# Channel attention with its weights turned and applied to v, and the output weights applied after

## What is computed

```
q = jnp.einsum('bse,ef->bsf', x, Wq)
k = jnp.einsum('bse,ef->bsf', x, Wk)
v = jnp.einsum('bse,ef->bsf', x, Wv)
qT = jnp.swapaxes(q, 1, 2)
kT = jnp.swapaxes(k, 1, 2)
vT = jnp.swapaxes(v, 1, 2)
attn_scores = jnp.einsum('bes,bfs->bef', qT, kT) / np.sqrt(HEAD_DIM)
attn_weights = jax.nn.softmax(attn_scores, axis=-1)
attn_output = jnp.einsum('bef,bfs->bes', attn_weights, vT)
attn_output = jnp.swapaxes(attn_output, 1, 2)
return jnp.einsum('bse,ef->bsf', attn_output, Wo)
```

## Time and profile before

| | us |
|---|---|
| median of 3 executions (lowest, highest) | 1319.75 (1319.05, 1320.85) |
| the profiled execution | 1320.28 |
| its span, first to last instruction | 1318.3 |
| TensorE busy in it | 1182.8 (90%) |
| VectorE, ScalarE, GpSimd busy | 774.4, 580.5, 603.9 |

### The profile page before, as it was taken

How to read it: one execution, slowest core, us unless ns; L and a number is a source line. 1 busy time by engine, 2 the same in 40 slices (tenths; PEclk the granted TensorE clock), 3 DMA queues, 4 the chain that set the end, 5 groups by cost and what they waited for, 6 DMA issues and landing times. The chain is left out here.

```text
span 1318.3 us, 24667 instructions
## 1 busy us (share of the span) xinstructions
PE 1182.8 (90%) x7421; PEld 831.5 (63%) x7422; DVE 774.4 (59%) x1930; ACT 580.5 (44%) x1504; POOL 603.9 (46%) x752
## 2 busy tenths in 40 slices
PE   7997889967989869978999999999999759999995
PEld 5774556544555534446888888888888536666663
DVE  4553688865887749955667767767666422222221
ACT  3432676643333300016656766666676323333331
POOL 2001465533655537636556666656665112232322
PEclk9998999988999979979999999999999869999998
DMA  7000000002998030041000000000002212222323
GB/s 259 0 0 12 14 18 12 13 1 81 187 206 170 1 154 12 0 188 72 5 13 13 13 15 15 20 12 12 12 17 77 85 43 42 47 44 44 47 41 88
DMA packets 46354, 69.41 MB, mean 53 GB/s; under 512 B 4736, under 2 KB 42672, under 8 KB 45232
## 3 DMA queue, kind: packets, MB, share of 16 engines
q1 hardware_dynamic: 37136, 52.95, 15.1%
q0 software_dynamic: 7152, 9.34, 4.4%
q10 hardware_dynamic: 2000, 6.29, 1.3%
HBM read 57.12 MB, written 32.58 MB: 68 GB/s over the span
## 5 line engine op out<-in xcount | busy, mean ns | idle before, releaser
L1742 PE MATMUL ga.pkq<-ga.xnT,g.early 128*128 128x128 f32 x1280 | 157.0, 276 | 1.0 <-ACT ga.halves L1660 1.0
L1742 PEld LDWEIGHTS ga.pkq<-ga.xnT,g.early 128*128 128x128 f32 x1280 | 151.6, 193 | 9.6 <-issue 8.2
L1522 POOL TENSOR_TENSOR ga.halves<-ga.halves,g.ga_sinT 128x512 f32<-128x512 f32 x80 | 103.3, 1291 | 51.6 <-ACT ga.halves L1660 51.6
L1786 PE MATMUL ga.turn_out<-g.early,ga.aT 128*128 128x256 f32 x512 | 118.3, 385 | 0.3 <-ACT ga.aT L1682 0.3
L1667 ACT ACTIVATE ga.e<-ga.psc,ga.negmax 128x128 f32<-128x128 f32 x256 | 90.6, 366 | 46.9 <-DVE ga.negmax L1588 45.9
L1530 POOL TENSOR_TENSOR ga.kqT<-ga.by_cos,ga.halves 128x512 f32<-128x512 f32 x80 | 102.6, 1283 | 16.5 <-issue 16.5
L1786 PEld LDWEIGHTS ga.turn_out<-g.early,ga.aT 128*128 128x128 f32 x512 | 95.9, 192 | 12.7 <-ACT ga.aT L1682 0.7
L1897 DVE TENSOR_TENSOR ex.hidden<-ex.silu,ex.p 128x512 f32<-128x512 f32 x39 | 26.8, 687 | 124.3 <-PE ex.p L1950 117.9
L1575 DVE TENSOR_TENSOR ga.by_cos<-ga.pkq,g.ga_cosT 128x512 f32<-128x512 f32 x80 | 55.3, 691 | 72.5 <-PE ga.pkq L1742 44.6
L1767 PE MATMUL ga.paT<-ga.pT,ga.v 128*128 128x512 f32 x128 | 68.4, 617 | 12.3 <-ACT ga.pT L1675 9.1
L1945 PE MATMUL ex.p<-g.spare,ex.xnT 128*128 x156 | 76.9, 616 | 1.1 <-ACT ex.xnT L1925 0.8
(11 more groups left out here) (290 smaller groups left out, 2630.2 us busy)
## 6 DMA issues: line engine op xcount, KB each, us to landing
mo_rows<-in_pad_rows SPq DMA_DIRECT2D x1, 18447.0 KB, 101.4
ex.row<-mo_rows SPq DMA_DIRECT2D x39, 129.0 KB, 2.1
g.spare<-in_mo_w SPq DMA_DIRECT2D x1, 4096.0 KB, 12.1
g.late<-in_mo_w SPq DMA_DIRECT2D x1, 4096.0 KB, 22.7
g.early<-in_mo_w SPq DMA_DIRECT2D x1, 4096.0 KB, 12.4
g.ctxT<-in_ctxR SPq DMA_DIRECT2D x1, 2048.0 KB, 11.9
xa.ctxT<-in_ctxT SPq DMA_DIRECT2D x16, 128.0 KB, 2.5
g.spare<-cv_rows SPq DMA_DIRECT2D x1, 2048.0 KB, 8.0
```

Source lines behind the costliest of these rows:

```text
L1522: nc.gpsimd.tensor_tensor(by_sin[:, par, :].rearrange("p (h t) -> p h t", h=REP), halves[:, par, :].rearrange("p (h t) -> p h t", h=REP), ...
L1742: last = nc.tensor.matmul(pkq[:, par, j * P:(j + 1) * P], w[:, q, at * P:(at + 1) * P], xnT[:, s.par, q, :], start=(q == 0), stop=(q == C ...
L1786: last = nc.tensor.matmul(pout, aT[:, h // REP, (h % REP) * P:(h % REP + 1) * P], g.ga_wo[:, h, :], start=(h == 0), stop=(h == H - 1))
```

## The change

The product over `f` is now taken with v first. After the exponentials of batch s-1, TensorE turns the 256x256 matrix `w` in four transposes into the new PSUM tile `pwT`, and VectorE copies it to `wT` (128x512, one instruction). One step later TensorE multiplies `wT` and `vT` into `pmix` (now attention output by channel, four matmuls of 128 columns); ScalarE scales its rows by the inverted sums into `mixed` (two instructions of 128x128); then TensorE multiplies `mixed` by the output weights into `pout`. Gone are the product `w` x `wo`, VectorE's scaling of the output weights and the 128x512 copy `mix`.

```diff
--- before.py
+++ after.py
@@ -264,21 +264,21 @@
         xnT = m.sb("xnT", [P, 2, C, P])
         qk = m.sb("qk", [P, 2, 2 * D])
         vT = m.sb("vT", [P, 2, C, P])
-        w = m.sb("w", [P, 2, C, D])
+        w, wT = m.sb("w", [P, 2, C, D]), m.sb("wT", [P, 2, C, D])
         negmax, rowsum = m.sb("negmax", [P, 2, C]), m.sb("rowsum", [P, 2, C])
-        wo = m.sb("wo", [P, 2, C, D])
-        mix = m.sb("mix", [P, 2, C, D])
+        mixed = m.sb("mixed", [P, 2, C, P])
         turn = m.ps("turn", [P, 512])
         pqk = m.ps("pqk", [P, 2 * D])
         pv = m.ps("pv", [P, 512])
         psc = m.ps("psc", [P, C, D])
-        pmix = m.ps("pmix", [P, C, D])
+        pwT = m.ps("pwT", [P, C, D])
+        pmix = m.ps("pmix", [P, 512])
         pout = m.ps("pout", [P, 512])
         (var_ready, rstd_ready, xn_ready, turned, xnT_ready, qk_done, qk_ready, vT_done, vT_ready, scores_done,
-         max_ready, w_ready, wo_ready, mix_done, mix_ready, out_done, x_added) = map(m.sem, (
+         max_ready, w_ready, sum_ready, w_turned, wT_ready, mix_done, mix_ready, out_done, x_added) = map(m.sem, (
             "var_ready", "rstd_ready", "xn_ready", "turned", "xnT_ready", "qk_done", "qk_ready", "vT_done",
-            "vT_ready", "scores_done", "max_ready", "w_ready", "wo_ready", "mix_done", "mix_ready", "out_done",
-            "x_added"))
+            "vT_ready", "scores_done", "max_ready", "w_ready", "sum_ready", "w_turned", "wT_ready", "mix_done",
+            "mix_ready", "out_done", "x_added"))
         g.finished = m.sems
         scale = 8 ** -0.5
         block = ctx.enter_context(nc.Block())
@@ -341,16 +341,18 @@
                 b = s.back(1)
                 if b.on:
                     dve.wait_ge(w_ready, upto(b))
-                    nc.vector.reciprocal(rowsum[:, b.par, :], rowsum[:, b.par, :])
-                    dve.drain()
-                    if b.base is None and b.n == 0:
-                        dve.wait_ge(g.ca_o_loaded, 16)
+                    nc.vector.reciprocal(rowsum[:, b.par, :], rowsum[:, b.par, :]).then_inc(sum_ready, 1)
+                if s.on:
+                    dve.wait_ge(vT_done, upto(s))
+                    if s.past(2):
+                        dve.wait_ge(mix_done, upto(s, back=2))
+                    nc.vector.tensor_copy(vT[:, s.par, :, :], pv[:, 0:D]).then_inc(vT_ready, 1)
+                b = s.back(1)
+                if b.on:
+                    dve.wait_ge(w_turned, upto(b))
                     if b.past(2):
                         dve.wait_ge(mix_done, upto(b, back=2))
-                    for c in range(C):
-                        last = nc.vector.tensor_scalar(wo[:, b.par, c, :], g.ca_wo[:, c, :], rowsum[:, b.par, c:c + 1],
-                                                       None, ALU.mult)
-                    last.then_inc(wo_ready, 1)
+                    nc.vector.tensor_copy(wT[:, b.par, :, :], pwT[:]).then_inc(wT_ready, 1)
                 b = s.back(-2)
                 if b.on and b.base is None and b.n in X_PARTS:
                     dve.wait_ge(g.x_loaded[X_PARTS.index(b.n)], 16)
@@ -359,11 +361,6 @@
                     if b.past(2):
                         dve.wait_ge(xn_ready, upto(b, back=2))
                     layer_norm_stats(nc, m, g.x[:, b.i, :], b.par, var_ready)
-                if s.on:
-                    dve.wait_ge(vT_done, upto(s))
-                    if s.past(2):
-                        dve.wait_ge(out_done, upto(s, back=2))
-                    nc.vector.tensor_copy(vT[:, s.par, :, :], pv[:, 0:D]).then_inc(vT_ready, 1)
             steps(dve, step, 2, 2)
 
         @block.scalar
@@ -374,11 +371,22 @@
                     if s.past(2):
                         act.wait_ge(vT_done, upto(s, back=2))
                     nc.scalar.activation(xnT[:, s.par, :, :], turn[:, 0:D], ACT.Copy).then_inc(xnT_ready, 1)
+                b = s.back(2)
+                if b.on:
+                    act.wait_ge(mix_done, upto(b))
+                    act.wait_ge(sum_ready, upto(b))
+                    if b.past(2):
+                        act.wait_ge(out_done, upto(b, back=2))
+                    for c in range(C):
+                        last = nc.scalar.activation(mixed[:, b.par, c, :], pmix[:, c * P:(c + 1) * P], ACT.Copy,
+                                                    scale=rowsum[:, b.par, c:c + 1])
+                    last.then_inc(mix_ready, 1)
                 b = s.back(1)
                 if b.on:
                     act.wait_ge(max_ready, upto(b))
                     if b.past(2):
-                        act.wait_ge(mix_done, upto(b, back=2))
+                        act.wait_ge(w_turned, upto(b, back=2))
+                        act.wait_ge(mix_ready, upto(b, back=2))
                     for c in range(C):
                         last = nc.scalar.activation(w[:, b.par, c, :], psc[:, c, :], ACT.Exp, bias=negmax[:, b.par, c:c + 1],
                                                     scale=scale, accum_out=rowsum[:, b.par, c:c + 1])
@@ -388,11 +396,6 @@
                     if s.past(2):
                         act.wait_ge(scores_done, upto(s, back=2))
                     nc.scalar.activation(qk[:, s.par, :], pqk[:], ACT.Copy).then_inc(qk_ready, 1)
-                if b.on:
-                    act.wait_ge(mix_done, upto(b))
-                    if b.past(2):
-                        act.wait_ge(out_done, upto(b, back=2))
-                    nc.scalar.activation(mix[:, b.par, :, :], pmix[:], ACT.Copy).then_inc(mix_ready, 1)
             steps(act, step, 0, 2)
 
         @block.tensor
@@ -418,14 +421,15 @@
                     last.then_inc(scores_done, 1)
                 b = s.back(2)
                 if b.on:
-                    pe.wait_ge(mix_ready, upto(b))
+                    pe.wait_ge(wT_ready, upto(b))
                     pe.wait_ge(vT_ready, upto(b))
                     if b.past(1):
-                        pe.wait_ge(x_added, upto(b, back=1))
+                        pe.wait_ge(mix_ready, upto(b, back=1))
                     for c in range(C):
-                        last = nc.tensor.matmul(pout[:, 0:D], vT[:, b.par, c, :], mix[:, b.par, c, :],
-                                                start=(c == 0), stop=(c == C - 1))
-                    last.then_inc(out_done, 1)
+                        for f in range(C):
+                            last = nc.tensor.matmul(pmix[:, c * P:(c + 1) * P], wT[:, b.par, f, c * P:(c + 1) * P],
+                                                    vT[:, b.par, f, :], start=(f == 0), stop=(f == C - 1))
+                    last.then_inc(mix_done, 1)
                 if s.on:
                     pe.wait_ge(xnT_ready, upto(s))
                     if s.base is None and s.n == 0:
@@ -435,6 +439,18 @@
                     for c in range(C):
                         last = nc.tensor.matmul(pqk[:], xnT[:, s.par, c, :], g.ca_wqk[:, c, :], start=(c == 0), stop=(c == C - 1))
                     last.then_inc(qk_done, 1)
+                b = s.back(2)
+                if b.on:
+                    pe.wait_ge(mix_ready, upto(b))
+                    if b.base is None and b.n == 0:
+                        pe.wait_ge(g.ca_o_loaded, 16)
+                    if b.past(1):
+                        pe.wait_ge(x_added, upto(b, back=1))
+                    for c in range(C):
+                        last = nc.tensor.matmul(pout[:, 0:D], mixed[:, b.par, c, :], g.ca_wo[:, c, :],
+                                                start=(c == 0), stop=(c == C - 1))
+                    last.then_inc(out_done, 1)
+                if s.on:
                     if s.base is None and s.n == 0:
                         pe.wait_ge(g.ca_v_loaded, 16)
                     if s.past(1):
@@ -446,14 +462,13 @@
                     last.then_inc(vT_done, 1)
                 b = s.back(1)
                 if b.on:
-                    pe.wait_ge(wo_ready, upto(b))
+                    pe.wait_ge(w_ready, upto(b))
                     if b.past(1):
-                        pe.wait_ge(mix_ready, upto(b, back=1))
+                        pe.wait_ge(wT_ready, upto(b, back=1))
                     for f in range(C):
                         for c in range(C):
-                            last = nc.tensor.matmul(pmix[:, f, :], w[:, b.par, c, f * P:(f + 1) * P], wo[:, b.par, c, :],
-                                                    start=(c == 0), stop=(c == C - 1))
-                    last.then_inc(mix_done, 1)
+                            last = nc.tensor.transpose(pwT[:, f, c * P:(c + 1) * P], w[:, b.par, c, f * P:(f + 1) * P], g.ident[:])
+                    last.then_inc(w_turned, 1)
             steps(pe, step, 0, 2)
```

## The result

| | before | after |
|---|---|---|
| median of the runs, first set (6 each) | 1319.78 us | 1309.80 us |
| lowest to highest | 1319.05 to 1324.1 | 1307.63 to 1311.29 |
| profiled execution, its span | 1320.28, 1318.3 | 1307.63, 1305.8 |

The ratio is 0.9917, with a 95% interval of 0.9900 to 0.9933: faster by 0.8%, 8.8 to 13.2 us. Taken of the 1319.75 us from which the forecast started, that is 1308.8 us. The forecast was 1312.0, with a range from 1309.5: the sign was right, the gain is some 3 us larger, and it lies just past the range's lower end. The changed kernel was run twice more (`again` 0.9923 [0.9909, 0.9938], `again2` 0.9931 [0.9915, 0.9946]). Over all sets the mean of 92 runs of before is 1320.3 and that of 17 runs of after 1309.9: **10.5 us, give or take 0.8**.

What follows compares the result with a forecast made beforehand. TensorE's own work was taken to bound channel attention. First steps -3.6, ten steps -4.1 and last steps 0 made -7.7 us, for a median of 1312.0 us, range 1309.5 to 1316.5.

Steps and rivals of the forecast that it cites:

- TensorE sets the stage's time, its own work is the price: Steady channel attention: TensorE busy all 62 us from 37 to 99; other engines' work is free if ready in time.
- The step, 5.87: Steady channel attention: -1.73 + 0.89 + 0.43 = -0.41 us a step, from 6.28 to 5.87; ten steps give 4.1.
- the room of 0.13: Steady step: VectorE's copy wT lets TensorE start at 6.82 for pmix's slot at 6.95; cost 0 to 0.10, taken as 0.
- The addition and `turn`: Steady step: addition and normalising end at 5.50, the next turn wants it at 5.87; room 0.1 to 0.3 us.
- The first steps, -3.6: Start of channel attention, to turn of batch 5: 4.18 us earlier less 0.6 for a disturbance, so 3.6 gained.
- the clearing, for which 0.6 was allowed: First steps: GpSimd's clearing may hold VectorE's small scaling and normalising of batch 3; 0.6 us, bounds 0 and 1.2.
- The last steps, 0: From turn of batch 15 to the last addition: one more link, each shorter; 14.6 against 14.55, change 0 +-0.5 us.
- The sum for the stage: Channel attention: -3.6 first steps, -4.1 ten steps, 0 last steps, in all -7.7 us.
- "Later stages ... shift as a whole", 1 to 2 us: Stages after channel attention: same instructions, no gain of their own; clock rises may move them a microsecond or two.
- A: Rival: in every step copy wT or the normalising comes 0.1 to 0.3 late; 1313.4 to 1315.5 us; chance 0.26.
- B: Rival: transposes of w cost as matmuls, 0.89 for four, a step of 6.33; about 1318 us; chance 0.07.
- C: Rival: transposes don't hold the clock up, so it falls inside channel attention; about 1341 us; chance 0.05.

Runs made afterwards that it cites:

- early: Changed kernel with the transposes of w ahead of the v group and copy wT ahead of vT, in all steps; 1310.74 us.
- warm: Twelve unused f32 matmuls added early in cross-attention: to the kernel before (1316.77, again 1317.37 us), the changed one (1310.12, again 1308.84) and `ahead` (1308.45).
- pad4: Changed kernel with the four transposes of w issued twice in every step, same result; 1317.4 us, ratio 0.9976.
- cut: Kernel before with one of the four matmuls of the product of weights left out, order and waits kept; 1314.39 us, ratio 0.9952.
- ahead: Changed kernel with the transposes of w ahead of v and copy wT ahead of vT only from the fourth step on; 1312.72 us.
- tailfill: Kernel before with four unused f32 matmuls in TensorE's 2.02 us wait ahead of the last product; 1318.72 us, ratio 0.9985.

## Why the prediction was right, and where it was wrong

- **TensorE sets the stage's time, its own work is the price.** Right: no gap from 37 to 99 us, before or after.
- **The step, 5.87.** 5.905 measured. Transposes 0.44 for 0.43, new product 0.89 for 0.89. Of the missing 0.035, 0.02 is the copy `wT`, as `early` shows: 0.69 as taken, but the room of 0.13 didn't cover the early weight load in every second step. 0.01 is the transposes, and the rest is rounding. The prediction took 0 for the copy and kept 0.10 for the range; it was a fifth of that. All together it is 0.33 us in ten steps.
- **The addition and `turn`.** Right: the normalising ends at 39.27, and `turn` starts at 39.54 without idle time; only behind the clearing did it wait, 0.28.
- **The first steps, -3.6.** `turn` of batch 5 came at 33.66, where 36.91 - 3.6 = 33.31 was forecast. It isn't the clearing, for which 0.6 was allowed: from `turn` of batch 2 (15.56) it is 18.10, forecast 3 x 5.87 + 0.6 = 18.21. It is the very first step, taken as unchanged: its v group was drawn 1.34 long (1.05 before), with more idle time at its weight load for which the trace names no cause, and v of batch 1 started at 14.24 instead of 13.80. No term had that, and most of it is this execution's: the same code has `turn` of batch 1 at 11.44 in this profile and at 11.19 and 11.15 in `again` and `again2`.

```profile
10.26 1.34 PE L460 MATMUL ca.pv<-ca.xnT,g.early 128*128 128x128 f32 x8
10.26 1.15 PEld L460 LDWEIGHTS ca.pv<-ca.xnT,g.early 128*128 128x128 f32 x7 [0.52 <-issue]
```

- **The last steps, 0.** Right: 92.69 + 14.53 = 107.22, forecast 14.6 from `turn` of batch 15, before 14.55.
- **The sum for the stage.** -7.7 forecast, -6.94 measured: 0.35 in the first steps, 0.33 in the ten steps, 0.14 between the addition and the next stage, less a few hundredths. All within the bounds that the terms had. Over the other profiles the stage's gain is 7.3 (+-0.5), with which the forecast agrees.
- **"Later stages ... shift as a whole", 1 to 2 us.** This is the step that failed, and it carries the miss. The stage's gain came out 0.8 smaller than forecast (0.4 by all profiles), and the whole 2.8 larger (10.5 for 7.7), so the later stages gave 3.5 (3.2), where the sum had nothing. The size of this term was taken from three runs that lay within 1.8 us. 92 runs lie between 1316.4 and 1324.6, with a standard deviation of 2.1: three runs said too little. And the earlier trace rows already showed what could move: a clock of 0.50 and TensorE busy for all of the 2 us at 118 to 120, so a stretch in which low clock is paid for in full. What the change gave there was worked out as nothing, since its instructions are the same. But the stage that ends in front of it wasn't, and the `warm` kernels show that the clock at this opening depends on the work that TensorE is given there.
- **Rivals.** A was right in its mechanism and wrong in its price (0.02 a step, not 0.1 to 0.25). B and C are refuted, C also in `pad4` with ten transposes a step. The Trainium skill's rule in "TensorE: Matmul & The Clock Gate", section "Part 4: PE-mode transpose", that the full clock doesn't engage for transposes, doesn't carry over to transposes strewn among f32 matmuls: the granted clock was 1.00 throughout the steps of both kernels, with six and with ten transposes in a step.

**What stays open.** Why the changed stage leaves the clock better off than the old one. `pad4` and `cut` together show that it goes with the new order and not with the length of the stage; which part of the order does it isn't shown. The wait of 2.02 us and GpSimd's pause were tried alone and together and give 1.1 (+-1.2); `cut`, with the old end and an early start, has the low clock in full; `ahead`, with the new end, kept only some 0.2 of the 3.5, with one low stretch of 10.2 us at the opening in its profile. So the length of the low clock at this one opening doesn't give the time by itself: the openings of linear and of grouped attention move as well. No experiment touched those two.

## What to carry to other kernels

Where one engine is busy without a gap, the price of a change can be summed from the starts of its groups, to 0.04 us a step here; reassociating a product paid here because four matmuls of 0.43 us gave way to four of 0.22 and four transposes of 0.11. The term that such a sum can't see is what the next stage's opening does with the clock: look there for low-clock stretches with TensorE busy, and give them 2 to 4 us of range on either side, not the spread of three runs. When a result is to be understood to a microsecond, take the stage's own gain from the start of the next stage, in several profiles (the same stage differed by up to 2.6 us between them), and keep it apart from the total. And compare the mean granted clock of all executions of both kernels: here it gives the size of the rest.

## What the runs showed of the hardware

- Two more semaphore clears in GpSimd's stream move a pause of 0.52 us from the first reciprocal root to one 50 us later, and two fewer bring it back. So here the place of the pause hung on how many clears stand in the stream; whether other instructions move it as well wasn't tried.
- In the first steps GpSimd's clearing of SBUF held VectorE instructions that work on SBUF alone until about its end: the scaling of 128x2 took 2.02 us beside a clearing of 1.85 and ended 0.03 after it, and takes 0.17 elsewhere; the normalising took 1.07 beside one of 1.02 and ended 0.13 after it, and takes 0.41 elsewhere. The maximum, which reads PSUM, took its usual 0.69 beside a clearing in before's trace.
- The same kernel spreads over 8 us (1316.4 to 1324.6, 92 runs), and its time goes with its low clock (correlation 0.84, 0.31 us for each microsecond). Twelve matmuls that compute nothing, put where TensorE waits, make it 2.6 us (+-1.0) faster.
- `turn` of batch 1 starts anywhere from 11.0 to 13.05 us in seven profiles of the same stage code; in `tailfill`, the latest, TensorE waits 1.59 us for the first weights, and in before 0.47 for ScalarE alone.
